# Routing an expert layer: all experts for every row, or two passes with rows scattered by expert

## The reference, cut to what matters

```
f = layernorm(x)                                   # 4096 x 128
H = gelu(f @ W1 + b1)                              # W1 128 x 512, so H is 4096 x 512
probs = softmax(H @ Wg + bg)                       # 8 experts
assign = argmax(probs)                             # one expert for each row
for e in range(8):
    y = H @ Wd[e] + bd[e]                          # Wd[e] 512 x 128
    out += where(assign == e, probs[:, e] * y, 0)
x = x + out
```

## Time and profile before

| | us |
|---|---|
| median of 3 runs | 1527.73 |
| lowest, highest run | 1526.89, 1830.92 |
| span of the profiled execution | 1525.2 |
| what lies around the span (median less span) | 2.5 |
| PE busy | 1371.0 (90%) |
| DVE busy | 1327.9 (87%) |
| ACT busy | 1091.3 (72%) |
| POOL busy | 713.4 (47%) |

### The profile page before, as it was taken

The page is one execution under the profiler, slowest core; times in us unless marked ns, Lnnn a source line. Parts: engine busy times, 40 slices in busy tenths (PEclk is TensorE's granted clock), DMA queues, the critical chain, the costliest instruction groups (busy, mean ns, idle before and its releaser), DMA issues. The chain is left out here.

```text
span 1525.2 us, 28287 instructions
## 1 busy us (share of the span) xinstructions
PE 1371.0 (90%) x8095; PEld 839.0 (55%) x8155; DVE 1327.9 (87%) x2378; ACT 1091.3 (72%) x1737; POOL 713.4 (47%) x950
## 2 busy tenths in 40 slices
PE   5599999999959999999999767999999996899998
PEld 4344444444428888888888753444444442455544
DVE  5789999999979999999999866899999997567665
ACT  6477777777739999999999655887887774434240
POOL 4144545455539999999999650223233332000000
PEclk9799999999989999999999988999999999899999
DMA  6055555555400000000000022555555550000000
GB/s 246 1 179 186 194 189 193 190 193 183 147 0 1 0 0 0 0 0 0 0 0 0 0 111 83 195 193 191 193 193 193 193 193 28 1 15 8 14 8 14
DMA packets 27312, 142.07 MB, mean 93 GB/s; under 512 B 2297, under 2 KB 10626, under 8 KB 10754
## 3 DMA queue, kind: packets, MB, share of 16 engines
q1 hardware_dynamic: 27266, 141.49, 26.3%
HBM read 139.39 MB, written 2.10 MB: 93 GB/s over the span
## 5 line engine op out<-in xcount | busy, mean ns | idle before, releaser
L882 PE MATMUL r_p_y<-w_ffn,r_z_t 128*128 128x128 f32 x1920 | 253.2, 275 | 26.5 <-ACT r_z_t L919 23.0
L882 PEld LDWEIGHTS r_p_y<-w_ffn,r_z_t 128*128 128x128 f32 x1920 | 253.4, 192 | 6.2
L992 POOL TENSOR_TENSOR r_stat<-r_stat,minus_half 128x4 f32<-128x4 f32 x240 | 242.0, 1008 | 18.8
L582 DVE SCALAR_TENSOR_TENSOR b_prob<-b_adj,b_prob 128x1024 f32<-128x1024 int32 x128 | 188.1, 1473 | 24.6 <-ACT b_prob L502 24.3
L538 POOL TENSOR_TENSOR b_lo<-b_prob,b_hi 128x1024 f16<-128x1024 f32 x32 | 79.9, 2498 | 257.2 <-ACT b_hi L509 257.2
L582 DVE SCALAR_TENSOR_TENSOR a_prob<-a_adj,a_prob 128x1024 f32<-128x1024 int32 x128 | 182.1, 1422 | 20.3 <-ACT a_prob L502 20.3
L502 ACT ACTIVATE b_prob<-b_p_s,shift,g_unit 128x1024 f32<-128x1024 f32 x128 | 154.0, 1203 | 52.3 <-PE b_p_s L438 52.1
L502 ACT ACTIVATE a_prob<-a_p_s 128x1024 f32<-128x1024 f32 x128 | 131.0, 1023 | 73.9 <-PE a_p_s L438 73.9
L951 DVE BATCH_NORM_STATS2 r_parts<-r_z 128x6 f32<-128x256 f32 x480 | 182.2, 422 | 1.3 <-ACT r_z L906 1.3
L944 DVE SCALAR_TENSOR_TENSOR r_h<-r_tanh,r_p_y 128x512 f32<-128x512 f32 x240 | 164.4, 685 | 4.1 <-ACT r_tanh L902 1.6
L538 POOL TENSOR_TENSOR a_lo<-a_prob,a_hi 128x1024 f16<-128x1024 f32 x32 | 81.6, 2551 | 181.1 <-ACT a_hi L509 181.1
(11 more groups left out here) (247 smaller groups left out, 3081.9 us busy)
## 6 DMA issues: line engine op xcount, KB each, us to landing
a_adj<-in_adj_t SPq DMA_DIRECT2D x64, 1024.0 KB, 4.8
b_adj<-in_adj_t SPq DMA_DIRECT2D x64, 1024.0 KB, 4.8
x_rows<-in_x SPq DMA_DIRECT2D x4, 512.0 KB, 7.2
wd_raw<-in_wd SPq DMA_DIRECT2D x1, 2048.0 KB
out_x<-e_acc SPq DMA_DIRECT2D x8, 256.0 KB, 2.3
late<-in_late SPq DMA_DIRECT2D x1, 756.0 KB
early<-in_early SPq DMA_DIRECT2D x1, 192.0 KB, 3.7
rows<-in_rows SPq DMA_DIRECT2D x1, 1.5 KB
```

What stands on the lines that cost most here:

```text
L582: nc.vector.scalar_tensor_tensor(prob[st][:], adj[transfer % ADJ][:, st % 2, :], 0.0, prob[st][:], ALU.is_gt, ALU.mult).then_inc(s["masked ...
L882: last = nc.tensor.matmul(out[:, D * t:D * t + D], z_t[g % R][:, P * t:P * t + P], k.w_ffn[:], start=False, stop=(t == TPC - 1), skip_grou ...
L992: nc.gpsimd.tensor_tensor(stat[g][:, 1, :], stat[g][:, 0, :], k.minus_half[:], ALU.pow)\
```

## The change

`experts` becomes two functions, each a block with its own programs.

`choose_experts` (first pass) goes over the 8 chunks: rows, transposes, hidden blocks and gelu as before, but no halves of the gelu; the logits come from the float32 gelu and float32 Wg in 16 matmuls per chunk. DVE forms a one-hot choice in bf16; PE counts with it, by 14 small matmuls against a triangular matrix and ones (`ranks`), how many earlier rows took the same expert; DVE turns that into a row address (`places`). A packed row holds f (128), x (128), tag, gate and two zeros: 260 float32. POOL writes each tile's 128 packed rows by an indirect DMA to `k.sorted` in HBM, at expert * 4096 + rank. At the end DVE computes for 40 tiles which expert and which rows each takes (`table`).

`run_experts` (second pass) goes over 10 groups of 4 tiles. SP reads each tile's row address from SBUF into a register and loads the tile. PE reads the tile's expert into a register and multiplies by that expert's weights alone, 12 matmuls that move 128 columns and a float32 matmul for the bias. ACT makes the gelu, POOL its high halves, DVE the low halves. DVE forms gate * y + x, and POOL writes each tile's rows to the output by an indirect DMA; rows whose tag is out of bounds (blanks) are dropped.

`k.sorted` is first filled with blank rows by 8 transfers on SP's queue in `recurrence`: 32,896 rows of 1040 bytes. POOL waits for them before its first scatter. `prepare_weights` scales the biases of the experts and makes two constant matrices; it no longer splits Wg. `normalise_a` gets a memset of `k.bd` on DVE, a wait before its load on SP, and five iotas on POOL. `k.g_rows` moves to a shorter life.

The diff, cut (`choose`, `weigh`, `table` and semaphore waits that repeat the pattern are left out):

```diff
 normalise_a
+            for to, of in ((k.late[:], io["late"]), (k.rows[:], io["rows"]), (k.wd[:], io["wd"])):
+                sp.dma_start(to, of).then_inc(k.late_in, 16)
+            sp.wait_ge(preset, 1)
+            sp.dma_start(k.bd[0:1, :], ...).then_inc(k.late_in, 16)
 prepare_weights, vector
-            nc.vector.tensor_scalar(wg, wg, k.e_scale[:, 2:3], None, ALU.mult)
-            nc.vector.tensor_copy(wg_hi, wg)
-            nc.vector.tensor_tensor(wg_lo, wg, wg_hi, ALU.subtract)
+            nc.vector.tensor_scalar(k.bd[:], k.bd[:], k.e_scale[:, 0:1], k.e_scale[:, 1:2], ALU.mult, ALU.mult)
+            nc.vector.tensor_scalar(k.before_row[:], k.before_row[:], 0.0, None, ALU.is_gt)
+            nc.vector.tensor_scalar(k.upto[:], k.upto[:], 0.0, None, ALU.is_ge)
+            nc.vector.memset(k.blank[:], 0.0)
+            nc.vector.memset(k.blank[:, TAG:TAG + 1], NOWHERE)
 recurrence, sync
+            for i in range(BLANKS):
+                sp.dma_start(rows[:, each * i:last, :], k.blank[:]...broadcast_to(...)).then_inc(k.blanked, 16)
 choose_experts
+        tensor:
+            turn_rows(0)
+            hidden(0)
+            for c in range(CHUNKS):
+                if c + 1 < CHUNKS:
+                    turn_rows(c + 1)
+                logits(c)
+                if c + 1 < CHUNKS:
+                    hidden(c + 1)
+                ranks(c)
+        scalar:
+            front(0)
+            gelus(0)
+            for c in range(CHUNKS):
+                if c + 1 < CHUNKS:
+                    front(c + 1)
+                    gelus(c + 1)
+                exps(c)
+        vector:
+            def rows(c):
+                if c > 1:
+                    dve.wait_ge(sent[c % 2], 16 * TPC * (c // 2))
+                    dve.wait_ge(s["ft_ready"], c - 1)
+                for t in range(TPC):
+                    last = normalised(k, pack[c % 2][:, t, 0:D], c, t)
+                last.then_inc(s["f_ready"], 1)
...
+            for c in range(CHUNKS):
+                if c + 1 < CHUNKS:
+                    rows_low(c + 1)
+                choose(c)
+                weigh(c)
+                places(c)
+                if c + 2 < CHUNKS:
+                    rows(c + 2)
+            table()
+        gpsimd:
+            pool.wait_ge(k.blanked, 16 * BLANKS)
+            for c in range(CHUNKS):
...
+                nc.gpsimd.tensor_copy(pack[par][:, :, D:2 * D], k.x[:, TPC * c:TPC * c + TPC, :])
+                pool.wait_ge(s["to_row"], c + 1)
+                for t in range(TPC):
+                    nc.gpsimd.indirect_dma_start(k.sorted, ...to_row[par][:, t:t + 1]..., pack[par][:, t, :])
+                        .then_inc(sent[par], 16)
 run_experts
+        sync, for each group q and tile t:
+                    row = sp.value_load(routed[0:1, j:j + 1], ...)
+                    sp.dma_start(got[q % RING][:, t, :], k.sorted[ds(row, P), :])
+        tensor:
+            def product(q, t):
...
+                own = ds(pe.value_load(order[0:1, j:j + 1], ...), D)
+                nc.tensor.matmul(out, k.ones[:], k.bd[:, own], start=True, stop=False)
+                for h in range(HC):
+                    nc.tensor.matmul(out, hi, w_hi, ...)
+                    nc.tensor.matmul(out, hi, w_lo, ...)
+                    last = nc.tensor.matmul(out, lo, w_hi, ...)
+            for q in range(GROUPS):
+                if q + 1 < GROUPS:
+                    hidden(q + 1)
+                for t in range(TPC):
+                    product(q, t)
+                if q + 2 < GROUPS:
+                    turn_rows(q + 2)
+        scalar, for each q:
+                gelus(q)          # block h waits for lo_ready of block h of q - 1
+                front(q + 1)
+        vector:
+            for q in range(GROUPS):
+                if q + 1 < GROUPS:
+                    for h in range(HC):
+                        lows(q + 1, h)
+                if q + 2 < GROUPS:
+                    rows_low(q + 2)
+                finish(q)
+        gpsimd:
+            def highs(q):
+                for h in range(HC):
+                    pool.wait_ge(s["gelu_ready"], HC * q + h + 1)
...
+                    nc.gpsimd.tensor_scalar(hid_hi[q % 2][:, h, :], hid[h][:], k.e_scale[:, 0:1], None, ALU.mult)
+            def store(q):
+                pool.wait_ge(s["done"], q + 1)
+                for t in range(TPC):
+                    nc.gpsimd.indirect_dma_start(k.io["out"], ...to_row..., done[par][:, t, :], ..., bounds_check=N - 1)
+            highs(0)
+            for q in range(GROUPS):
+                if q + 1 < GROUPS:
+                    highs(q + 1)
+                store(q)
```

More of the change, by code:

```diff
@@ L55 @@
 S_MAX = 7.25
+REGION = N
+ROW = 2 * D + 4
+TAG, GATE = 2 * D, 2 * D + 1
+TILES = 40
+GROUPS = TILES // TPC
+NOWHERE = 2.0 * N
+BLANKS = 8
 EARLY = {"ident": D, "wkq_t": 2 * D}
@@ L1327, in _, with choose_experts @@
                     dve.wait_ge(s["unit_ready"], c + 1)
[L1330 removed]
+def choose_experts(k, order, routed):
     nc = k.nc
     with ExitStack() as ctx:
[L1337 to L1365, removed]
[L1366 to L1378 removed]
@@ L1443, in chunk @@
-            def chunk(c, par, first=False, last=False):
-                if not first:
-                    turn_gate(c, False)
-                if not last:
-                    turn_rows(c + 1, False)
-                for r in range(ROUNDS):
-                    product(c, par, first, r)
-                    if r == 0 and first:
-                        turn_gate(c, True)
-                    if r == 0:
-                        biases(c, first)
-                    if last:
-                        continue
-                    for h in HIDDEN[r]:
-                        hidden(c + 1, h, False)
-                    if r == LOGITS:
-                        logits(c + 1, 1 - par, False)
@@ L1461, in _, with ranks @@
-            turn_rows(0, True)
-            for h in range(HC):
-                hidden(0, h, True)
-            logits(0, 0, True)
-            chunk(0, 0, first=True)
-            chunk(1, 1)
-            with pe.Fori(1, CHUNKS // 2 - 1) as cc:
-                chunk(2 * cc, 0)
-                chunk(2 * cc + 1, 1)
-            chunk(CHUNKS - 2, 0)
-            chunk(CHUNKS - 1, 1, last=True)
+            def ranks(c):
+                pe.wait_ge(s["choices"], c + 1)
+                if c > 0:
+                    pe.wait_ge(s["taken"], c + 1)
+                hot = one_hot[c % 2]
+                for t in range(TPC + 1):
+                    if t < TPC:
+                        nc.tensor.matmul(p_rank[:, t, :], k.before_row[:], hot[:, t, :], start=True, stop=(t == 0))
+                    for u in range(t):
+                        last = nc.tensor.matmul(p_rank[:, t, :], k.ones_bf[:], hot[:, u, :], start=(t == TPC and u == 0),
+                                                stop=(u == t - 1))
+                last.then_inc(s["rank_ready"], 1)
@@ new lines, in _ @@
+            for i in range(2):
+                nc.vector.memset(pack[i][:, :, GATE + 1:ROW], 0.0)
+            nc.vector.tensor_copy(taken[:], k.region[:]).then_inc(s["taken"], 1)
+            rows(0)
+            rows(1)
+            rows_low(0)
+            for c in range(CHUNKS):
+                if c + 1 < CHUNKS:
+                    rows_low(c + 1)
+                choose(c)
[3 more added lines that the diff above has]
+                    rows(c + 2)
@@ L1607, in _ @@
             rows_low(0)
[L1608 removed]
             for h in range(HC):
[L1610 to L1619 removed]
+                lows(0, h)
+            rows_low(1)
@@ L1622, in build, with experts @@
+def experts(k):
+    with ExitStack() as span:
+        order, routed = (k.sb("x_" + n, [P, TILES], I32, span) for n in ("order", "routed"))
+        choose_experts(k, order, routed)
+        run_experts(k, order, routed)
 def build(nc, io):
```

450 lines of the change are left out of this document (276 added, 174 removed).

## The result

The changed kernel takes 1646.0 us (median of 4 runs, 1645.4 to 1650.7), the kernel before 1527.6 us in the same series: a ratio of 1.0781 [1.0765, 1.0797]. The profiled execution has a span of 1643.6 us against 1525.2, so 118.4 us more. One of the four executions of the kernel before took 1830.9 us, far above the others, and is not in the ratio. The forecast was 1603 in a range of 1550 to 1685, with 0.87 on slower: 75 us more were forecast, 118 came.

What follows compares the result with a forecast made beforehand. PE bounded the experts before; afterwards loops through POOL's scatters bound both passes. First pass to 1472, second pass 127, `prepare_weights` 1: span 1600, median 2.5 above, so 1603 us, range 1550 to 1685.

Steps and rivals of the forecast that it cites:

- Start and first addresses: First pass: last gelu at 1305.5, logits 5, then 9.9 for the rest of a turn; addresses of chunk 0 at 1320.
- Six turns of the first pass: First pass: scatters, rows, logits, gelus and addresses follow one another in a loop of 23.3 us, taken six times, to 1460.
- Its end: End of first pass: chunk 7 takes 5 us for choosing, counting and placing, 6.3 for its scatter, 1 for the border: 1472.
- Fill: Start of second pass: loads 4, then transposes, casts, hidden blocks, gelus up to the last high half: 13 us.
- Group 1: 7, without a scatter: Second pass, after the fill: group 1 was to take 7 us, with no scatter in it.
- Eight turns: Second pass: POOL's loop of four high halves at 1.15, four scatters at 1.0 and a 3.05 wait, 11.7 us: 94.
- the 27 us in the total: Second pass: low halves on DVE holding off POOL's high halves, 3 us more a group; left in the upper range.
- An indirect DMA at 2.1: Both passes: each indirect DMA costs POOL 2.1 us, 1.1 more than assumed; +70, 1673; chance 0.14.
- PE at half clock in the second pass: Second pass: the clock stays at half, PE's loop is 15.7 us, 4 more than POOL's; +33, 1636; chance 0.12.
- All low ends: Both passes: scatters 0.45, high halves 0.41, logits at full clock; 1542, no change to be measured; chance 0.10.
- A first pass that overlaps: First pass: one chunk's scatter lies beside the next chunk, 7.3 us a chunk at PE's pace; 1483; chance 0.03.
- Blanks that don't fit: Blank-row transfers at 50 GB/s hold up the second attention's first loads by 245 us; 1848; chance 0.03.

Runs made afterwards that it cites:

- the kernel with the cheap copy: The changed kernel with POOL's high halves made by a plain copy to float16, the multiplication by the scale left out: 1625.1 us, ratio 1.0638.
- the fastest kernel: The loosened kernel with six buffers, rows one more chunk ahead, exponentials and ranks a step later, and logits moving 512 columns: 1494.6 us, ratio 0.9785.
- the loosened kernel: The changed kernel with five first-pass buffers and earlier rows, ScalarE's high halves, four second-pass load buffers and earlier transposes: 1498.1 us, ratio 0.9816.

## Why the prediction was right, and where its sizes were off

The case that I took for likeliest is what happened, in both passes, and the sign was right. The signs that I named came: transposes 23.9 us apart behind a DMA, logits at 0.50, POOL's one long gap in a group of 3.29 us, no idle time ahead of the second attention; only the groups are 14.35 apart and not 12. But the size was not right: the span ended 43.6 us above the sum of 1600, and the change cost 118 us where I had 75. The range took it in because its upper part stood there for two rivals, neither of which happened. By its steps:

- **Start and first addresses.** 1320 predicted; the last address instruction ends at 1320.02. The sum is right, in part by luck: the last gelu ends 0.9 us later than I had it, and the part behind the logits takes 8.7 and not 9.9.
- **Six turns of the first pass.** 23.3 predicted, 144.1 / 6 = 24.0 measured: +4 in all, and +1 until POOL starts its first scatter behind the first addresses. Scatters 3 x 1.27 + 0.98 and a landing of 1.5 behind them are 6.3, as predicted. Logits were 6.83 for 6.4, the gelu's table was hidden behind them (so -1.3), and the gelus waited for hidden blocks that were partly still at half clock (+1). POOL starts 0.8 us behind the addresses in every turn, which I had at nothing, and the small DVE steps took 1.55 for 2.0. That the turn came within 0.7 us is partly luck: terms off by a microsecond cancelled.
- **Its end.** 12 us from the scatter of chunk 6 to the border predicted, 16.0 measured: +4. The four scatters of chunk 7 started 5.85 us behind those of chunk 6, for which I had 5 of choosing and placing; in fact POOL's own queue set it, the four scatters of chunk 6 and the copy behind them. They took 4.8 us for 4.0, and the queue of loads began at 1481.19, 5.4 us behind the last scatter's end, for which I had a landing of 2.3 and 1 for the border.
- **Fill.** Up to the last high half of group 0 13 predicted, 16.4 measured: +3.4. The loads take 5.3 us for 4, and the four highs follow one another at 1.55, slower than the gelus that I let set their pace.
- **The first turn of the second pass.** "Group 1: 7, without a scatter" is the one step that failed in its mechanism and cost much. POOL's order has the scatters of group 0 behind the high halves of group 1, so this is a whole turn of the loop: 1497.6 to 1517.0, 19.4 us. It also has a wait of 3.82, as `rows_low(1)` stands on DVE behind all low halves of group 0 and PE's next hidden blocks wait for it, and one of 4.45 before the scatters. +12.4.
- **Eight turns.** 11.7 predicted, 14.3 measured: +20. Of the 2.65 a turn, 4 x (1.55 - 1.15) = 1.6 are the high half, and 4.88 - 4.0 = 0.9 the scatters: the instruction has the predicted 0.98, but 0.30 lies between two of them. The wait was 3.29 for 3.05.
- **Drain.** 13 predicted, 12.3 measured.

+5, +4, +3.4, +12.4, +20, -0.7 make 44; the 1 us that I added for `prepare_weights` lies within the 1320.

The high half was the worst of the sizes: I took the row of a two-input instruction on 508 columns, 1.15, over the multiplication of 512 columns in place, 2.02. The latter is nearest in kind (a factor from a small tensor), and the measured 1.55 lies between.

**The rule on SBUF.** In the change DVE's low half takes 1.17 us beside a high half of POOL, and 0.75 in the last of each group and in every one of the kernel with ScalarE's high halves. POOL's high half takes 1.55 to 1.56 beside a low half and 1.59 as the first of a group, with none beside it. So DVE pays 0.42 us and POOL nothing, and the 27 us in the total didn't come. The Trainium skill, "SBUF — State Buffer", section "Who interferes with whom", has the two exclude each other. The trace agrees that they disturb one another, but not for a whole instruction: the low half from 1518.6 to 1519.8 lies inside POOL's high half from 1518.5 to 1520.1. In the kernel with the cheap copy both pay: of the four copies of a group three take 0.64 us and one 1.10, and low halves take up to 1.62. There DVE's time set the wait; in the change it is hidden behind POOL.

**Register loads.** In the chain, SP's loads of a group start 1.1 us apart, of which 0.33 is the issue and 0.46 the two instructions of the line that reads the row number (L1629). It costs 3 us once, in the fill, and nothing in the turns of the change. The Trainium skill, "DMA: Bandwidth & Descriptors", section "Latency and other measured facts", has a floor of some 0.6 us. The 0.46 is somewhat less; and the 10.9 us that the rule gave for PE's loop did not come, since the second pass of the fastest kernel takes 8.1 us a turn with the same loads.

**The rivals.** An indirect DMA at 2.1: no, 0.98 and 0.30. PE at half clock in the second pass: the clock was low (0.64 and 0.76), the bound was not PE. Its 1636 us are nearer to the measured time than my 1603, by accident. All low ends: no. A first pass that overlaps: not in the change, but in the kernels whose rows don't wait for the addresses it is about what came, 6.9 to 7.4 us for a steady chunk and 7.1 and 7.8 on average, where the rival had 7.3. Blanks that don't fit: no.

So the gain of a third less PE work went to two places. 99 us lie in the first pass: its two buffers, the order of the queues around them and the slow logits in their wake, of which three buffers with the rows made earlier give back 65. The high halves on POOL cost 38.5 us with the rest as it was, and 51.5 once the rest is loose. With both gone, the scattered rows are 1527.3 - 1494.6 = 32.7 us faster than the kernel before.

## What to carry to other kernels

Two buffers overlap nothing if the refill of one waits until that same one is empty and the next chunk's work stands in the queues behind the refill: write the ring of waits down before counting engine time. An engine that issues indirect DMAs like these pays 1.2 to 1.3 us for each; put elementwise work in its queue only if the sum of both, and of the wait between them, is below the turn of the others. And look at the granted clock of each stretch before a price is carried from one order of work to another: the same logits cost PE 6.83 us in the change and 3.64 in the loosened kernel.

## What the runs showed of the hardware

- An indirect DMA of 128 rows keeps POOL for 0.96 to 1.04 us (1.3 to 1.5 in a few), the next starts 1.27 to 1.34 us behind it, and what it moves lands 2.1 to 3.4 us behind its start, 2.3 to 2.5 in the middle (the change).
- POOL's multiplication by a scalar from a tensor, 128x512 float32 to float16, takes 1.55 to 1.60 us; its plain copy with the same change of type 0.61 to 0.65, and 1.10 for one of four beside DVE's low halves; a copy in float32 0.61 to 0.63.
- PE can be busy without a gap and stay at half clock: 9.96 of 10.00 us at 0.50 in the kernel with three buffers (1330 to 1340). It can also fall from 1.00 to half while it is busy: in the kernel with both passes loosened behind the logits of 8 columns, at 1316, 1323 and 1333, and not between 1340 and 1361, with the same logits. With the logits turned round, 512 columns, it stayed at 1.00 from 1306 to 1358. What decides between these, the runs don't settle.
- A float32 product with 128x128 weights and 8 columns is two instructions; each costs PE 0.114 to 0.119 us at full clock (3.64 / 32, 2.49 / 21) and 6.83 / 32 = 0.213 at half.
